# Two output biases by one bf16 matmul a half in PSUM, in place of two VectorE passes

## What is computed

```python
h0 = gelu(h @ W0a.T + b0a);  out0 = h0 @ W0b.T + b0b
h1 = relu(h @ W1a.T + b1a);  out1 = h1 @ W1b.T + b1b
mask0 = (argmax(h @ Wg.T) == 0)          # first expert for this token
x = x + gb * (out0 * mask0 + out1 * (1 - mask0))
```

## Time and profile before

| | |
|---|---|
| median of three runs | 604.27 us |
| the profiled execution | 601.1 us |
| its span, first to last instruction | 599.3 us |
| TensorE (PE) busy | 520.9 us, 87% |
| VectorE (DVE) busy | 480.9 us, 80% |
| ScalarE (ACT) busy | 365.5 us, 61% |
| GpSimd (POOL) busy | 309.7 us, 52% |

### The profile page before, as it was taken

The page is one execution under the profiler, slowest core; times in us unless marked ns, Lnnn a source line. Parts: engine busy times, 40 slices in busy tenths (PEclk is TensorE's granted clock), DMA queues, the critical chain, the costliest instruction groups (busy, mean ns, idle before and its releaser), DMA issues.

```text
span 599.3 us, 14257 instructions
## 1 busy us (share of the span) xinstructions
PE 520.9 (87%) x4912; PEld 446.5 (75%) x4912; DVE 480.9 (80%) x949; ACT 365.5 (61%) x521; POOL 309.7 (52%) x300
## 2 busy tenths in 40 slices
PE   5435757999898989999999999999999999999874
PEld 4324545788787878787878888788979788888774
DVE  3548255779798989899898999899999899887572
ACT  2424644868575866667676858585766667675320
POOL 6334223455554665655656555556665655552441
PEclk9856696999999999999999999999999999999997
DMA  8835252433516080715244251708080715210100
GB/s 246 208 39 83 25 91 55 78 67 59 104 34 128 2 161 1 128 32 93 66 67 92 48 111 28 131 5 154 0 161 2 136 26 91 53 39 2 36 19 18
DMA packets 43802, 43.74 MB, mean 73 GB/s; under 512 B 5344, under 2 KB 40800, under 8 KB 43760
## 3 DMA queue, kind: packets, MB, share of 16 engines
q1 hardware_dynamic: 43760, 43.19, 37.2%
HBM read 13.39 MB, written 4.23 MB: 29 GB/s over the span
## 4 chain that ended last, share of the span: by engine, by line
PE 31%; DVE 29%; DMA 14%; issue 11%; POOL 6%; ACT 4%; SPq 3%; DVEq 1%; POOLq 0%; ACTq 0%
DVE mx L933 8%; DMA xs<-x 7%; DMA qs<-mx_rows 4%; PE ps_s L382 4%; PE ps_t L401 3%; DVE z L872 3%; SPq L282 2%; DMA qs<-parts_q 2%; POOL xs L1186 2%; PE ps_c L333 2%; PE ps_t L405 2%; DVE hid L1079 2%; PE ps_o L333 2%; ACT score_rows L794 2%; PE ps_c L335 2%
## 5 line engine op out<-in xcount | busy, mean ns | idle before, releaser
L794 ACT ACTIVATE score_rows<-ps_s 128x1024 f32<-128x1024 f32 x96 | 98.9, 1031 | 78.2 <-PE ps_s L382 59.8
L1246 POOL TENSOR_SCALAR_AFFINE_SELECT score_rows<-score_rows 128x512 f32<-128x512 f32 (+1 forms) x96 | 83.0, 865 | 101.8 <-ACT score_rows L794 101.8
L933 DVE TENSOR_REDUCE mx<-score_rows 128x4 f32<-128x1024 f32 (+1 forms) x96 | 114.0, 1210 | 4.4 <-POOL score_rows L1246 4.3
L806 ACT ACTIVATE p<-ps_t 128x1024 f32<-128x1024 f32 x96 | 98.4, 1025 | 16.9 <-PE ps_t L405 16.7
L382 PE MATMUL ps_s<-ks,qs 96*128 96x256 bf16 (+1 forms) x512 | 62.6, 259 | 19.6 <-DMA qs<-parts_q 15.9
L401 PE MATMUL ps_t<-qs,ks 99*128 99x256 bf16 (+1 forms) x512 | 60.7, 253 | 15.2 <-DMA qs<-mx_rows 14.3
L1186 POOL TENSOR_TENSOR xs<-z,xs 128x512 f32<-128x512 f32 (+1 forms) x16 | 30.7, 1922 | 61.7 <-DVE z L1022 61.7
L382 PEld LDWEIGHTS ps_s<-ks,qs 96*128 96x128 bf16 x512 | 36.8, 103 | 32.0 <-DMA qs<-parts_q 17.2
L401 PEld LDWEIGHTS ps_t<-qs,ks 99*128 99x128 bf16 x512 | 38.0, 100 | 23.1 <-DMA qs<-mx_rows 10.3
L856 DVE BATCH_NORM_STATS2 ln_st<-xs 128x6 f32<-128x256 f32 (+1 forms) x64 | 23.9, 415 | 35.2 <-DMA xs<-x 27.7
L1234 POOL TENSOR_TENSOR hid_lo<-hid,hid_hi 128x512 fp32r<-128x512 f32 x32 | 42.8, 1351 | 4.8 <-DVE hid_hi L1092 4.8
(11 more groups left out here) (166 smaller groups left out, 1648.1 us busy)
## 6 DMA issues: line engine op xcount, KB each, us to landing
qs<-parts_q SPq DMA_DIRECT2D x96, 128.0 KB, 3.9
ks<-parts_k SPq DMA_DIRECT2D x96, 128.0 KB, 4.4
xs<-x SPq DMA_DIRECT2D x16, 256.0 KB, 5.3
gates<-gates_scratch SPq DMA_DIRECT2D x16, 256.0 KB, 4.6
out<-xs SPq DMA_DIRECT2D x16, 256.0 KB, 3.5
p<-wmod SPq DMA_DIRECT2D x1, 1024.0 KB, 6.3
p<-waT SPq DMA_DIRECT2D x1, 1024.0 KB, 8.7
p<-wmod SPq DMA_DIRECT2D x1, 512.0 KB, 5.2
```

The costliest lines, as they stand in the source:

```text
L794: act.activation(score_rows[c % 2][:], ps_s[:], ACT.Copy).then_inc(scores_out, 1)
L806: act.activation((p0, p1)[tile][:, h0:h0 + n, :], ps_t[:].rearrange("p (h s) -> p h s", h=n), ACT.Exp, scale=SCALE).then_inc(exp_done, 1)
L933: dve.tensor_reduce(dst, score_rows[c % 2][:].rearrange("p (h k) -> p h k", h=n), AX_X, ALU.max).then_inc(max_done, 1)
L1246: pool.affine_select(out=diag, in_=diag, compare_op=ALU.is_ge, fill=NEG, base=0, pattern=[[0, n], [-1, P]], channel_multiplier=1).then_inc ...
```

## The change

The two bias passes on VectorE (L971, L974) go, and the semaphores behind them: `picked` now says that y is whole. In their place TensorE starts each of the two banks with one matmul, before the first expert's products, which then accumulate onto it. Its stationary operand `share` is 128 x 128 of 1/32, its moving one `bias_rows`, 128 x 512 bf16: 32 rows of the bias rounded to bf16, 32 of the rest, 32 of the rest of that, 32 of zeros. `split_bias` makes both once, on VectorE in its second step. The float32 bias is loaded into y, which isn't used before, and the mask constant `past` that lay there has a tile of its own.

```diff
@@ -100,7 +100,9 @@
         wa = [sb(f"wa{i}", [P, KT, F], F32R) for i in range(2)]
         wb = [sb(f"wb{i}", [P, FT, D], F32R) for i in range(2)]
         bias_a = sb("bias_a", [P, FT])
-        bias_b = sb("bias_b", [P, 2 * D])
+        share = sb("share", [P, P], BF16)
+        bias_rows = sb("bias_rows", [P, 2 * D], BF16)
+        past = sb("past", [P, P])
         ident = sb("ident", [P, P])
         ident_b = sb("ident_b", [P, P], BF16)
         past_b = sb("past_b", [P, P], BF16)
@@ -159,7 +161,7 @@
         wb_raw = [hid32[:].rearrange("p a b s -> p (a b) s"), oT[:]]
         wdq_raw, wuq_raw, wuv_raw, wg_raw = z2[:], attn[:], score_rows[0][:, 0:D], logits[:]
         cT_raw, c_silu = mx[:], mx_rest[:]
-        past = y[:, 0, 0:P]
+        bias_b = y[:].rearrange("p t d -> p (t d)")
         clamped, sign = [g[:].rearrange("p g d -> p (g d)")[0:NB] for g in gates]
 
 
@@ -188,8 +190,8 @@
             "gate_done logit_rows_ready gate_turned logits_ready first_ready choice_ready".split())
         up_done, gelu_done, relu_done, hid_hi_ready, lo_gelu_ready, lo_relu_ready = (sem(n) for n in
             "up_done gelu_done relu_done hid_hi_ready lo_gelu_ready lo_relu_ready".split())
-        dn_done, second_ready, picked, biased, y_ready, scaled, out_ready = (sem(n) for n in
-            "dn_done second_ready picked biased y_ready scaled out_ready".split())
+        dn_done, second_ready, picked, bias_split, scaled, out_ready = (sem(n) for n in
+            "dn_done second_ready picked bias_split scaled out_ready".split())
         st1, mv1, ve1, rs1, st2, mv2, ve2, rs2 = (sem(n) for n in
             "st1 mv1 ve1 rs1 st2 mv2 ve2 rs2".split())
         x_in, gates_in, stored = (x_in0, x_in1), (gates_in0, gates_in1), (stored0, stored1)
@@ -308,7 +310,7 @@
                 sp.dma_start(wb_raw[k], wbT[half, :].rearrange("(k p) f -> p k f", p=P)).then_inc(ffn_in, 16)
             sp.dma_start(wg_raw, wgT.rearrange("(k p) f -> p k f", p=P)).then_inc(ffn_in, 16)
             sp.dma_start(bias_a[:], ba).then_inc(ffn_in, 16)
-            sp.dma_start(bias_b[:], bb.to_broadcast([P, 2 * D])).then_inc(ffn_in, 16)
+            sp.dma_start(bias_b, bb.to_broadcast([P, 2 * D])).then_inc(ffn_in, 16)
 
             def step(at):
                 stack_q(at(1), 2)
@@ -581,11 +583,15 @@
                 pe.wait_ge(hid_hi_ready, 4 * b.n + 2 * e + 2)
                 pe.wait_ge((lo_gelu_ready, lo_relu_ready)[e], 2 * (b.n + 1))
                 bank_left(users)
+                if e == 0:
+                    if b.first and t == 0:
+                        pe.wait_ge(bias_split, 9)
+                    pe.matmul(BANK[f"DN{t}"][:], share[:], bias_rows[:], start=True, stop=False)
                 dst = BANK[f"DN{t}"][:, e * D:(e + 1) * D]
                 tok = slice(t * P, (t + 1) * P)
                 for n in range(e * FT // 2, (e + 1) * FT // 2):
                     mm = product(dst, (hid_hi[:, n, tok], hid_lo[:, n, tok]), (wb[0][:, n, :], wb[1][:, n, :]),
-                                 n == e * FT // 2, n == (e + 1) * FT // 2 - 1)
+                                 False, n == FT - 1)
                 mm.then_inc(dn_done, 1)
 
 
@@ -904,6 +910,26 @@
                 dve.wait_ge(clamp_ready, 3)
                 dve.scalar_tensor_tensor(out=clamped, in0=clamped, scalar=LEAST_GATE, in1=sign, op0=ALU.max, op1=ALU.mult).then_inc(clamp_ready, 1)
 
+            def split_bias(b):
+
+                if not b.first:
+                    return
+                one, two, three = slice(32, 64), slice(64, 96), slice(96, 128)
+                dve.wait_ge(ffn_in, 16 * 7)
+                dve.memset(share[:], 1.0 / 32).then_inc(bias_split, 1)
+                dve.tensor_copy(bias_rows[:], bias_b).then_inc(bias_split, 1)
+                dve.wait_ge(bias_split, 2)
+                for rows in (one, two):
+                    dve.tensor_tensor(bias_b[rows], bias_b[rows], bias_rows[rows, :], ALU.subtract).then_inc(bias_split, 1)
+                dve.wait_ge(bias_split, 4)
+                for rows in (one, two):
+                    dve.tensor_copy(bias_rows[rows, :], bias_b[rows]).then_inc(bias_split, 1)
+                dve.wait_ge(bias_split, 6)
+                dve.tensor_tensor(bias_b[two], bias_b[two], bias_rows[two, :], ALU.subtract).then_inc(bias_split, 1)
+                dve.wait_ge(bias_split, 7)
+                dve.tensor_copy(bias_rows[two, :], bias_b[two]).then_inc(bias_split, 1)
+                dve.memset(bias_rows[three, :], 0.0).then_inc(bias_split, 1)
+
             def late_low_part(b, n):
 
                 if b.first:
@@ -967,13 +993,6 @@
                 dve.scalar_tensor_tensor(out=y[:, t, :], in0=BANK[f"DN{t}"][:, 0:D], scalar=first[b.parity][:, t:t + 1], in1=y[:, t, :],
                                          op0=ALU.mult, op1=ALU.add).then_inc(picked, 1)
 
-                dve.wait_ge(picked, 2 * b.n + t + 1)
-                dve.scalar_tensor_tensor(out=y[:, t, :], in0=bias_b[:, 0:D], scalar=first[b.parity][:, t:t + 1], in1=y[:, t, :],
-                                         op0=ALU.mult, op1=ALU.add).then_inc(biased, 1)
-                dve.wait_ge(biased, 2 * b.n + t + 1)
-                dve.scalar_tensor_tensor(out=y[:, t, :], in0=bias_b[:, D:2 * D], scalar=second[b.parity][:, t:t + 1], in1=y[:, t, :],
-                                         op0=ALU.mult, op1=ALU.add).then_inc(y_ready, 1)
-
             def part_rest(b, src, parts, rest, done, part_ready, rest_ready, third_ready):
 
                 if b.off:
@@ -1060,7 +1079,7 @@
                     return
                 dve.wait_ge(gate_turned, b.n + 1)
 
-                wait(dve, y_ready, 2 * (b.n - 1))
+                wait(dve, picked, 2 * (b.n - 1))
                 wait(dve, choice_ready, b.n)
                 dve.tensor_copy(logits[:], BANK["GX"][:, 0:2 * TT].rearrange("p (t e) -> p t e", e=2)).then_inc(logits_ready, 1)
                 dve.wait_ge(logits_ready, b.n + 1)
@@ -1145,6 +1164,7 @@
                 g_high(at(3))
                 row_max(at(1), 3)
                 late_low_part(at(1), 8)
+                split_bias(at(1))
                 add_first_expert(at(4), 1)
                 ckv_low(at(0))
                 q_rest(at(0))
@@ -1189,7 +1209,7 @@
 
                 if b.off:
                     return
-                pool.wait_ge(y_ready, 2 * (b.n + 1))
+                pool.wait_ge(picked, 2 * (b.n + 1))
                 for t in range(TT):
                     ins = pool.tensor_tensor(y[:, t, :], y[:, t, :], gates[b.parity][:, 1, :], ALU.mult)
                 ins.then_inc(scaled, 1)
```

More of the change, by code:

```diff
@@ L1161, in _ @@
             pool.tensor_copy(ident_b[:], ident[:]).then_inc(consts_ready, 1)
-            pool.memset(past, 0.0).then_inc(consts_ready, 1)
+            pool.memset(past[:], 0.0).then_inc(consts_ready, 1)
             pool.wait_ge(consts_ready, 4)
-            pool.affine_select(out=past, in_=past, compare_op=ALU.is_ge, fill=NEG, base=0,
+            pool.affine_select(out=past[:], in_=past[:], compare_op=ALU.is_ge, fill=NEG, base=0,
                                pattern=[[1, P]], channel_multiplier=-1).then_inc(consts_ready, 1)
             pool.wait_ge(consts_ready, 5)
-            pool.tensor_copy(past_b[:], past).then_inc(consts_ready, 1)
+            pool.tensor_copy(past_b[:], past[:]).then_inc(consts_ready, 1)
             def inverse_deviation(b, n):
```

## The result

The changed kernel takes 607.63 us (median of 20 runs, 602.65 to 610.93), the kernel before 601.93 us beside it (20 runs, 597.79 to 605.94). The two medians are 5.7 us apart; the ratio of the two kernels, with its 95% interval, is 1.0079 [1.0051, 1.0108], or +4.8 us (3.1 to 6.5), and by it I go. The forecast was +3.2 us, with no change by over 1% as the likeliest case. The profiled execution took 605.11 us, its span 603.3.

A forecast was written before the change was run, and what follows sets the result against it. A way round the loop through x's load and TensorE, not VectorE's bias passes, was taken to set the period. Start +2.8, loop 0 and end +0.4 on 604.27 us gave 607.5 us; range 598 to 612 (8 in 10).

The forecast's parts named there:

- likeliest case: Whole kernel: 601 to 610 us, chance 0.54; no change by over 1% got 0.67 in all.
- The bound: Loop: a way round through x's load and TensorE, without bias passes, sets the 32.18 us period; the other is 0.32 behind.
- Rival (a): Loop: VectorE is the bound after all, 0.7 us a period gained until TensorE stops it, 598 us; chance 0.14.
- The loop: Thirteen steps: x 0.2 us earlier and matmuls 0.2 us beyond cover cancel each period; 0 us, from −5.5 to +3.4.
- cover: TensorE's wait ahead of turning z2 hides 0.17 to 0.35 of the matmuls' 0.43 us, leaving 0.08 to 0.26 a period.
- two stack transfers are issued earlier, and the DMA queue ahead of x is shorter: Loop: parts_q comes 0.7 to 1.3 us earlier, so x lands 0.2 us earlier a period (0 to 0.5).
- Rival (b): Loop: the DMA queue gives more, x 0.5 us earlier each period, 602 us; chance 0.12.
- The start: split_bias ahead of ckv_low costs 4.0 us, the queue ahead of the query stack returns 1.2: +2.8, from 1.1 to 4.2.
- The end: Last three steps: matmuls cost 1.4 us, GpSimd's wait for two last passes saves 1.0: +0.4, from −0.6 to +0.9.
- Rival (c): Slower by over 1%: serial start 4.2, 0.26 a period uncovered, end 0.9; 612.8 us, decided at +6; chance 0.20.
- The signs that were named: Profile after: VectorE busy about 447, period within 0.3, x wait kept, new idle times, ckv_low at 54, scores at 67 to 68.
- The skill's rule: VectorE with two SBUF inputs and GpSimd exclude each other on shared ports, so each removed pass would also unblock GpSimd.

The follow-up runs named there:

- e1: Kernel before with both bias passes removed and nothing in their place, output biases left out: 605.37 against 603.14 us, ratio 1.0031.
- e5: Kernel before with the load of x issued right behind the step's first stack_q: 590.88 against 603.45 us, ratio 0.9803.
- e2: Changed kernel with split_bias moved behind first_normalise in the same step: 604.88 against 603.14 us, ratio 1.0012.
- e4: Kernel before, passes kept, plus the nine split_bias instructions at the changed kernel's place, results unused: 604.03 against 603.14 us, ratio 1.002.
- e7: Changed kernel with x issued early and split_bias moved behind first_normalise: 586.85 us, ratio to the kernel before 0.9726.
- e6: Changed kernel with the load of x issued right behind the step's first stack_q: 590.55 against 603.45 us, ratio 0.9778.
- e8: Kernel before with x issued early and both bias passes removed, nothing in their place, biases left out: 584.68 against 602.98 us, ratio 0.9699.
- e10: Second run of e7's program (changed kernel, x early, split_bias moved): 587.05 against 602.98 us, ratio 0.9746.
- e9: Second run of e5's program (kernel before, x early): 591.62 against 602.98 us, ratio 0.9819.
- e3b: Changed kernel with each bias matmul done twice at a share of 1/64, four 512-column matmuls a batch: 611.83 against 603.45 us, ratio 1.0122.

## Why the prediction was right

**The bound.** Right. The way round the loop that holds no pass (score chunk, mask, `gate_ffn`, issue of x, x, `project_out`, z2) sets the period, and e1 and e5 show it from both sides: the passes gone alone gave nothing, x issued early alone gave 12.6 us (with the maxima's load, which moved up with it). Rival (a), 598 us by VectorE as the bound, is refuted for this kernel. It comes true only once x is early, and then with 0.3 us a period and not with 0.7.

**The loop, forecast 0, measured +2.0 us (1.1 to 2.0 with the like kernels).** The mechanism was right and one term was not there. Matmuls beyond their cover: forecast 0.2 us a period, measured 0.1 (1.2 us in twelve periods), with the cover of 0.17 to 0.35 measured as some 0.3. x: forecast 0.2 us earlier, measured no earlier in any kernel without the passes: from its issue to VectorE's start on it 5.44 us after, 5.47 in e2 and 5.43 in e1, against 5.32 before and 5.42 in e4 (means of the seven periods). The step that failed is "two stack transfers are issued earlier, and the DMA queue ahead of x is shorter": with `parts_q` earlier, x still found the engines full when it was issued, as before, and nothing was won. The stretch of 1 us in which x is issued, before and after (DMA share and GB/s last):

```profile
313.00:314.00 1.00, 0.69 (x6) 0.48 (x5) 0.93 (x4) 0.43 (x1) 0.59 (x1) 1.00 1.14 131
```

```profile
318.00:319.00 1.00, 0.79 (x8) 0.54 (x6) 1.00 (x2) 0.34 (x1) 0.51 (x1) 1.00 1.11 126
```

The maxima's DMA now follows 1.37 us behind x instead of 1.81, but that x comes later by it isn't shown: e4, which has the passes, has the same 5.4 us. Rival (b), 602 us, leaned on the same step and falls with it.

**The start, forecast +2.8 us.** At the place for which it was worked out, the second batch's scores, it is 2.95 us. The terms were off in opposite ways: the nine instructions take 4.7 us instead of 4.0, and the queue gives back 1.8 instead of 1.2. The casts took 1.97 us for 1.7, the two fills 0.44 for the 0.3 that no row stood behind, the gaps 0.28 for 0.15, and the overlap was 0.1 and not 0.2. Up to mark 3 another 0.7 us is lost in the changed kernel, but in e4 0.6 is won back, so what follows the start is worth under a microsecond with either sign. e2 against the changed kernel, and e7 against e6, show that the cost lies in the place and not in the work.

**The end, forecast +0.4, measured −0.5 us.** Both terms were off, to the same side. The passes were put at 1.0 us and brought 1.2 to 1.5 (e1 and e8, without passes and matmuls, end 89.69 and 89.83 us behind mark 15, the kernels with passes at the clock's full level 91.07 to 91.20). The last y is whole 0.48 us after its start instead of three passes later, which is the 1.0; where the rest comes from wasn't followed. The matmuls were put at 1.4 us and took 0.8 to 1.0 (the kernels with them end at 90.62 to 90.70). I had counted part of them at half clock, which the trace before showed in the last step and the later ones don't.

**The sum.** 2.8 + 0 + 0.4 was forecast, 3.7 + 2.0 − 0.5 = 5.2 measured in the stages, 4.8 in the runs. The errors stayed within the range, and the verdict was that of the likeliest case. That the forecast of 607.5 and the median of 607.63 agree so closely is luck of the base: it started at 604.27 us from three runs, where twenty gave 601.93. The change itself was forecast at +3.2 and is +4.8, 1.6 us more. Rival (c), over +6 us, would have needed 4.2 at the start and 0.1 a period; it had 3.7 and up to 0.17 (2.0 us in 12 periods), and so came near.

**The signs that were named.** VectorE's busy time 445.7 us (447 was forecast); period +0.20 (within 0.3); idle time ahead of the last maximum alone, of `g_hi` and of `rest_q`, where I had written of the last two maxima and the picks; the wait for x in every period; the turn of z2 right behind the score chunk; `ckv_low` at 55.3 rather than 54 (0.5 of it the first loads' later arrival in this execution); the scores at 68.4, a little later than 67 to 68 for the same reason.

**The skill's rule.** The rule quoted ahead (Trainium skill, "SBUF — State Buffer", section "SBUF: two separate sides") would have given GpSimd time back. GpSimd's busy time did fall from 309.7 to 307.8 us, and in e10 it was 308.7 against 311.0 in e9: 0.03 to 0.04 us for each of the 64 passes. Little of it lies on the way round the loop: from the score chunk to `gate_ffn` it took 2.50 us before and in e9, 2.46 after and in e10 (means of the seven periods).

## What to carry to other kernels

A chain that runs through the most loaded engine isn't proof that it is the bound: look for a second way round the loop that doesn't touch it, and for an engine that waits each period for something that it doesn't delay itself. Here that something was a load that stood last in a queue, and issuing it earlier was worth more than all arithmetic saved; only then, and with `split_bias` moved as well, did the saved arithmetic pay (−4.4 us, where the same moved `split_bias` without the early x gave +0.7). And one-time work has a price by its place: the same nine instructions cost 3 us ahead of the first q parts and nothing a few instructions later.

## What the runs showed of the hardware

- **TensorE's early rate.** The first group of 16 matmuls of 16 columns (L362 or L364, at 7 to 8 us) took 3.56 to 3.57 us in all twelve traces. The second, at about 15 to 16 us, took either 1.86 to 2.04 us (before, after, e4, e5, e10) or 3.43 us (the other seven). The clock column of the views says 1.00 for both, but the trace's first clock entry is only at 15.2 to 16.4 us in the five and at 23.0 to 25.6 us in the seven, so that column says nothing of the time ahead of it. The matmuls do. In e1, whose first entry is at 24.25 us, a 128x256 matmul took 0.41 us up to there and 0.28 us behind it; those are also the durations at the end of the kernel before at a granted clock of 0.50 and of 1.00. So TensorE began at the lower level and got the higher one at one of two times. It puts VectorE's first `rest_q` 4.4 us later in e1 than in the kernel before, about half of the 8 us between the lowest and the highest run of the kernel before. What decides it stays open. Before and e1:

```profile
15.11 1.92 PE L362 MATMUL ps_t<-mx_rest,p 128*128 128x16 f32 x16
```

```profile
15.49 3.43 PE L364 MATMUL ps_t<-mx_rest,p 128*128 128x16 f32 x16
...
23.83 0.41 PE L335 MATMUL ps_c<-h_hi,wq 128*128 128x256 f32 x1
...
24.38 0.28 PE L335 MATMUL ps_c<-h_hi,wq 128*128 128x256 f32 x1
```

- **Small VectorE operations beside GpSimd.** In the traces of before, after, e8, e9 and e10, from 60 us on, each 128x32 instruction of the maxima split does one of two things. If no GpSimd instruction runs as it starts, it takes 0.18 to 0.20 us (134 of 300). If one runs, it ends 0.04 to 0.09 us behind that one, however long this is, up to 1.23 us (the other 166). L972 above starts at 316.27 and ends at 317.42, 0.04 us behind the GpSimd instruction that began at 316.09. Taking VectorE work out moves the long ones to others, L972 and L974 (0.99 and 0.87 us in the mean of 16) instead of L941 and L943 (0.94 and 0.88), and doesn't shorten the four.

```profile
316.09 1.29 POOL L1224 TENSOR_TENSOR xs<-y,xs 128x512 f32 x1 [0.15 <-POOL y L1214]
317.34 1.17 POOL L1242 TENSOR_TENSOR parts_q<-rest_q,parts_q 128x512 bf16<-128x512 f32 x1
```

- **A load by its place in the queue.** The same 256 KB of x take 5.3 us in the median in the kernel before, 5.5 us in the changed one (5.3 in e1 and e2), and 3.4 us in e9 and e10, where they are issued ahead of most of the stack transfers:

```profile
xs<-x SPq DMA_DIRECT2D x16, 256.0 KB, 3.4
```

- **A 512-column bf16 matmul** adds 0.21 us to TensorE's stream where nothing covers it (0.41 for two, from e3b).
